# Attention exponentials in triples instead of pairs, with x kept in DRAM meanwhile

## What is computed

```python
q = (x @ Wq.T).reshape(d, n, h)          # d = 128 batches, n = 3327, h = 8
k = (x @ Wk.T).reshape(d, n, h)
v = (x @ Wv.T).reshape(d, n, h)
a = jnp.einsum('dnh,dmh->dnm', q, k) * scale
a = a + adj + adj
a = softmax(a, axis=2)
out = jnp.einsum('dnm,dmh->dnh', a, v).reshape(n, h * d) @ Wo.T
```

## Time and profile before

| | |
|---|---|
| median of three runs | 12,283.2 us |
| the profiled execution, its own time | 12,270.41 us |
| its span, first to last instruction | 12,268.5 us |
| TensorE matmul busy | 11,106.3 us (91%) |
| ScalarE busy | 10,590.3 us (86%) |
| VectorE busy | 10,190.5 us (83%) |
| GpSimd busy | 8,312.7 us (68%) |
| mean granted TensorE clock | 0.959 of 2.4 GHz |
| VectorE's adds (line 1011) | 9,216, 8,980.5 us |
| ScalarE's exponentials of sets (line 966) | 5,120, 7,345.2 us |
| ScalarE's exponentials of GpSimd blocks (line 961) | 4,096, 3,527.3 us |

### The profile page before, as it was taken

How to read it: one execution, slowest core, us unless ns; L and a number is a source line. 1 busy time by engine, 2 the same in 40 slices (tenths; PEclk the granted TensorE clock), 3 DMA queues, 4 the chain that set the end, 5 groups by cost and what they waited for, 6 DMA issues and landing times. The chain is left out here.

```text
span 12268.5 us, 378176 instructions
## 1 busy us (share of the span) xinstructions
PE 11106.3 (91%) x138208; PEld 5172.6 (42%) x138208; DVE 10190.5 (83%) x10283; ACT 10590.3 (86%) x9603; POOL 8312.7 (68%) x4135
## 2 busy tenths in 40 slices
PE   5759999999999999998999999998999999999743
PEld 4524444444444444444343344433343433444721
DVE  6358888888788888887888888888888888888388
ACT  3259999999899999998999999999999999998022
POOL 0017777777677777777777777777777777777023
PEclk7979999999899999999999999999999999999866
DMA  8773333333433333333333333333333333333522
GB/s 315 234 221 58 58 58 58 58 58 58 84 56 58 58 58 58 58 58 66 75 53 54 51 55 52 54 52 66 73 54 52 54 53 53 54 51 58 171 88 75
DMA packets 432583, 943.30 MB, mean 77 GB/s; under 512 B 100728, under 2 KB 349439, under 8 KB 381471
## 3 DMA queue, kind: packets, MB, share of 16 engines
q1 hardware_dynamic: 432508, 942.28, 39.4%
HBM read 799.88 MB, written 142.00 MB: 77 GB/s over the span
## 5 line engine op out<-in xcount | busy, mean ns | idle before, releaser
L1011 DVE SCALAR_TENSOR_TENSOR a_probs<-ps,a_adj 128x768 f32<-128x768 f32 (+1 forms) x9216 | 8980.5, 1020 | 1357.6 <-PE ps L904 1244.9
L986 POOL TENSOR_TENSOR a_pool_probs<-a_pool_probs,a_adj 128x768 f32<-128x768 f32 (+1 forms) x4096 | 8102.3, 1978 | 2382.1 <-ACT a_pool_probs L961 2382.1
L966 ACT ACTIVATE a_probs<-a_probs 128x1536 f32<-128x1536 f32 (+3 forms) x5120 | 7345.2, 1457 | 230.8 <-DVE a_probs L1011 199.8
L904 PE MATMUL ps<-a_q,a_k 34*128 34x512 f32 (+2 forms) x26624 | 4998.3, 413 | 416.0 <-DVE a_probs L1011 258.5
L921 PE MATMUL ps<-a_probs,a_v 128*9 128x192 f32 (+1 forms) x73728 | 4218.9, 341 | 5.3 <-ACT a_probs L966 4.0
L961 ACT ACTIVATE a_pool_probs<-ps 128x768 f32<-128x768 f32 (+1 forms) x4096 | 3527.3, 861 | 58.4 <-PE ps L904 37.4
L904 PEld LDWEIGHTS ps<-a_q,a_k 34*128 34x128 f32 x26624 | 2213.7, 185 | 3139.0 <-DVE a_probs L1011 1183.3
L921 PEld LDWEIGHTS ps<-a_probs,a_v 128*9 128x9 f32 x73728 | 1741.3, 90 | 1747.3 <-ACT a_probs L966 617.0
L921 PE MATMUL ps<-a_pool_probs,a_v 128*9 128x192 f32 (+1 forms) x32768 | 2222.3, 343 | 0.0
L921 PEld LDWEIGHTS ps<-a_pool_probs,a_v 128*9 128x9 f32 x32768 | 488.8, 88 | 1227.1 <-issue 1221.0
L1259 POOL TENSOR_TENSOR e_both<-e_tau,e_nat 128x3328 f32<-128x3328 f32 (+1 forms) x26 | 194.5, 7481 | 701.2 <-DVE e_tau L1297 701.2
(11 more groups left out here) (172 smaller groups left out, 2415.6 us busy)
## 6 DMA issues: line engine op xcount, KB each, us to landing
a_k<-k_parts SPq DMA_DIRECT2D x2048, 208.0 KB
a_v<-v_ext SPq DMA_DIRECT2D x512, 117.0 KB
adj_t<-tr SPq DMA_DIRECT2D x26, 1664.0 KB, 6.4
g0tile<-adj_t SPq DMA_DIRECT2D x26, 1664.0 KB, 6.9
g2tile<-adj_t SPq DMA_DIRECT2D x26, 1664.0 KB, 6.8
nat<-in_adj SPq DMA_DIRECT2D x25, 1663.5 KB, 10.3
e_nat<-in_adj SPq DMA_DIRECT2D x25, 1663.5 KB, 6.9
a_q<-q_parts SPq DMA_DIRECT2D x2048, 16.0 KB
```

The lines of the kernel that those rows point to most:

```text
L904: ins = nc.tensor.matmul(ps[:, slot + begin:slot + end], kt[row:row + SCORE_ROWS, P * j:P * (j + 1)].bitcast(F32R), qt[row:row + SCORE_ROW ...
L966: nc.scalar.activation(both, both, ACT.Exp, scale=2.0).then_inc(sums_exped, 1)
L986: nc.gpsimd.tensor_tensor(probs(k)[:, :, :], probs(k)[:, :, :], adj_c[:, :, j, :], ALU.mult).then_inc(multiplied, 1)
L1011: v.scalar_tensor_tensor(out=probs(k), in0=score(j).rearrange("p (i q) -> p i q", q=P), scalar=SCALE / 2, in1=adj_c[:, :, j, :], op0=ALU.m ...
```

## The change

`sets` is no longer built round the GpSimd blocks: the 18 blocks of VectorE are taken in their order, three at a time. So a batch has six exponentials of three blocks each: (0,2,3), (5,6,8), (9,11,12), (14,15,16), (18,19,21), (22,24,25). The ring still has four slots, now of three blocks (43,008 bytes a partition at 896 columns, 28,672 before). To make room, x is written to DRAM in `projection_phase`, its SBUF tile is freed after that phase, and `output_phase` loads it into a new tile. `weigh_at` follows from `sets`: it becomes {0,2,3} at step 3, {1} at 5, {4,5,6,8} at 8, {7} at 11, {9,11,12} at 12, {10} at 14, {14,15,16} at 16, {13} at 17, {17,18,19,21} at 21, {20} at 24, {22,23,24,25} at 25. The slots of scores, `ahead_by`, the GpSimd blocks and everything else stay.

```diff
+SET = 3
@@ projection_phase
+        x_stored = mem.sem("x_stored")
@@ SyncE of projection_phase
                 sp.dma_start(w[:, n], weight.rearrange("(c h) f -> c h f", h=HEADS)).then_inc(w_loaded, LOAD)
+            sp.dma_start(x_rows, keep.x[:, :, :]).then_inc(x_stored, LOAD)
             for u in range(units):
...
+            sp.wait_ge(x_stored, LOAD)
@@ attention_phase
     if n_pool:
-        alone = [(j,) for j in range(BLOCKS) if not any(abs(j - p) <= 1 for p in pool_blocks)]
-        sets = sorted([(p - 1, p + 1) for p in pool_blocks] + alone)
+        by_dve = [j for j in range(BLOCKS) if not by_pool[j]]
+        sets = [tuple(by_dve[n:n + SET]) for n in range(0, n_dve, SET)]
...
-        dve_ring = mem.sb(name + "probs", [P, ring, 2, nb, P])
+        dve_ring = mem.sb(name + "probs", [P, ring, len(sets[0]), nb, P])
@@ output_phase, SyncE
             sp.dma_start(w[:, :, :].rearrange("p c h -> p (c h)"), wo).then_inc(w_loaded, LOAD)
+            sp.dma_start(x[:, :, :], x_rows).then_inc(x_loaded, LOAD)
@@ output_phase, VectorE
             v.tensor_copy(w_t[:, :, :].rearrange("p h f -> p (h f)"), ps[:, 0:QCOLS]).then_inc(w_copied, 1)
+            dve.wait_ge(x_loaded, LOAD)
             with dve.Fori(0, BLOCKS // 2) as t:
@@ program
+    x_rows = scratch("x_rows", (P, BLOCKS, F))
...
+        with ExitStack() as x_stack:
+            keep.x = Memory(nc, x_stack).sb("x", [P, BLOCKS, F])
+            setup_phase(nc, keep, x, b0, b2, att_src, att_dst, o_rows)
...
+            projection_phase(nc, keep, (wq, wk, wv), (q_parts, k_parts), (q_norms, k_norms), v_ext, x_rows)
...
+        keep.x = Memory(nc, stack).sb("x_again", [P, BLOCKS, F])
+        output_phase(nc, keep, wo, o_rows, x_rows)
```

More of the change, by code:

```diff
@@ L390, in _, with projection_phase @@
             layer_norm_root(nc, act, norm)
-def projection_phase(nc, keep, weights, parts_of, norms_of, v_ext):
+def projection_phase(nc, keep, weights, parts_of, norms_of, v_ext, x_rows):
     with ExitStack() as stack:
@@ L1019, in _, with output_phase @@
                 finish(1, (c + 1) * BATCHES)
-def output_phase(nc, keep, wo, o_rows):
+def output_phase(nc, keep, wo, o_rows, x_rows):
     x = keep.x
@@ L1034, in output_phase @@
         norm = Norm(mem, "wo")
+        x_loaded = mem.sem("x_loaded")
         w_loaded, w_turned, w_copied = mem.sem("wo_loaded"), mem.sem("wo_turned"), mem.sem("wo_copied")
@@ L1333, in __init__ @@
         self.ps = mem.stack.enter_context(mem.nc.psum_tensor("ps", [P, 8 * BANK], F32))
-        self.x = mem.sb("x", [P, BLOCKS, F])
         self.ident = mem.sb("ident", [P, P])
@@ L1353, in program @@
         keep = Kept(Memory(nc, stack))
[L1354 to L1357, removed]
+        with ExitStack() as x_stack:
+            keep.x = Memory(nc, x_stack).sb("x", [P, BLOCKS, F])
+            setup_phase(nc, keep, x, b0, b2, att_src, att_dst, o_rows)
+            adjacency_phase(nc, keep, adj, adj_t)
+            gcn_phase(nc, keep, adj_t, w0, keep.deg0, keep.bias0, True)
+            projection_phase(nc, keep, (wq, wk, wv), (q_parts, k_parts), (q_norms, k_norms), v_ext, x_rows)
         with ExitStack() as bound_stack:
@@ L1374, in program @@
                 attention_phase(nc, keep, group, POOL_BLOCKS, adj_t, k_parts, q_parts, q_shift, v_ext, o_rows)
-        output_phase(nc, keep, wo, o_rows)
+        keep.x = Memory(nc, stack).sb("x_again", [P, BLOCKS, F])
+        output_phase(nc, keep, wo, o_rows, x_rows)
         gcn_phase(nc, keep, adj_t, w2, keep.deg2, keep.bias2, False)
```

## The result

The changed kernel takes 18,218.8 us (median of four runs, 18,190.2 to 18,230.7) against 12,294.0 us of the kernel before: 1.482 times as long, 95% interval 1.478 to 1.486. The forecast was 18,250 us, the range 16,150 to 19,700. The profiled run took 18,230.7 us.

The account below looks back on a forecast made before the run. The prediction took ScalarE, nearly always busy in attention, as the bound. It summed 1,940 + 10 + 256 x (32.6 + 31.1) = 18,257, say 18,250 us, range 16,150 to 19,700.

Parts of the forecast that it names:

- What bounds the kernel: Steady attention before the change: ScalarE busy 2346.51 of 2430 us and 2642.11 of 2680 us, 19.13 and 21.22 us per batch.
- The instructions: ScalarE in attention: six triples replace eight pairs and two singles, saving 195 us over 512 batches if ScalarE never waits.
- The ring: Attention: waits through all engines make batches of 29.64 and 26.20 us, adding 3,965 us at full clock.
- legs: Stretches from one triple's exponential to the next; wide tiles at full clock: 6.82, 3.40, 5.13, 6.82, 7.47 us.
- W's place: TensorE's weighing of a set, claimed to stand in front of the next scores; 1.25 us for three blocks in wide tiles.
- E's place: ScalarE's exponential of a set, claimed to stand ahead of a GpSimd block's exponential; 2.34 us for a wide triple.
- The clock: TensorE in attention: idle gaps bring 1.2 GHz, 42% of wide and 66% of narrow time; 32.6 and 31.1 us per batch.
- S(20): TensorE's scores of block 20; TensorE was forecast idle about 2 us before it in wide tiles.
- x in DRAM: Storing x after the projections and loading it for the output: 10 us taken, bounds 0 to 2 x 7.
- The signs to look for: Profile after: 3,072 set exponentials, ScalarE idle 3,500 us or more before them, TensorE waits, attention clock 0.6 to 0.9.
- Rival A: TensorE keeps full clock throughout attention, so the time is 16,250 us; chance 14%.
- Rival C: ScalarE stays the bound and grouping saves 195 us, giving 12,090 us, if the ring is under 20.9 us; chance 3%.

Follow-up runs that it names:

- kernel of nine pairs: Kernel before (x in SBUF) with nine pairs for eight pairs and two singles, other GpSimd blocks, new steps for exponentials and weighings: 12,160.1 us, ratio 0.9904.
- kernel with fillers: Changed kernel, with TensorE multiplying zeros into the accumulator ahead of the scores of blocks 7, 16 and 20: 16,801.2 us, ratio 1.368.
- the pairs: Changed kernel with VectorE's 18 blocks taken in order two at a time, ring of six slots of two blocks, x in DRAM: 16,850.8 us, ratio 1.372.
- the run with x alone: Changed kernel with the old eight pairs and two singles and a ring of pairs again, x still in DRAM: 12,296.1 us, ratio 1.0016.

## Why the prediction was right

**What bounds the kernel: right.** ScalarE was the bound and its cover was all but complete; the kernel of nine pairs, with ScalarE full, shows how little there was to gain.

**The instructions: right and small.** The triple takes 2,446 ns where 2.45 us was worked out, and no run contradicts 0.1 us for an instruction saved.

**The ring: right.** Forecast legs for wide tiles at full clock were 6.82, 3.40, 5.13, 6.82, 7.47 us. The trace has 6.65, 3.29 and 4.96 for the first three and, in the kernel with fillers, 6.66 and 7.41 for the fourth and the last; so each was put up to 0.2 us too high. A batch at full clock was put at 29.64 and 26.20 us and takes 28.96 and 25.71, the order's loss at 3,965 us and is 3,670. That W's place and E's place make the legs is shown by moving each. Size is not needed for a loss, as the pairs show, but it is a term of the legs: E is in them with 2.34 us for a triple and 1.59 for a pair.

**The clock: the mechanism right, its share too small.** I had put the low clock at 66% of the time in narrow and 42% in wide tiles. The granted clock of 0.64 means (1 - 0.64) / 0.5 = 72% and 0.72 means 56%. This share was chosen from stretches at the chunks' starts and not derived; it was the softest step. Low in both, it met legs that were put too long, and in narrow tiles its price was too high: with the measured shares and legs, the prediction's prices (33.6 and 36.6 us for a batch all low) give 31.4 us for a narrow and 33.2 for a wide batch. Forecast were 31.1 and 32.6, measured 30.3 and 33.3. The sum came within 0.2% because 256 x (-0.8 + 0.7) is close to zero, and not because each term was that good; that was luck. The pairs show how wide the real uncertainty was: there the same reasoning missed by 850 us beyond its upper end. The waits that were to pull the clock down were put somewhat long: 2 us ahead of S(20) and 1.6 ahead of S(16), where the timeline has 1.63 and 1.38. And the prediction took each long gap as the start of a low stretch; the gap of 1.38 us was followed by none, and in the kernel with fillers the clock fell without a gap over 0.5 us in the 8 us before. Fillers in TensorE's waits lower the share of low time; what else sets it stays open.

**x in DRAM: right.** 10 us, 0 to 14 forecast; 20 us, 0 to 39 measured.

**The signs to look for.** 3,072 exponentials of sets, an idle time before them of 5,018 us (3,500 or more forecast), waits of TensorE ahead of S(7) and S(20) for X, and a clock of 0.61 to 0.79 in attention (0.6 to 0.9 forecast) are all there. So is the wait ahead of S(16). Rival A (full clock, 16,250 us) was within 550 us of the kernel with fillers. Rival C (ScalarE stays the bound) is right for nine pairs and wrong for triples: the point from which it decides was put at 20.9 us for the ring.

The Trainium skill ("Perfetto Trace Analysis", Optimizing Scalar/DVE Operations) has beside its rule on grouping a second one: if ScalarE isn't saturated but causes bubbles on other engines, breaking instructions up may let work finish sooner. The triples turned the first case into the second, 99% busy into 64%, and breaking them up again in the run with x alone brought the time back to 12,296 us.

## What to carry to other kernels

Before grouping instructions on a full engine, write down for each engine its program order around the group, and follow from one grouped instruction to the next through every wait: if the round is longer than the engine's own work in it, grouping loses, however much overhead it saves. A small loss by order can bring a larger one when TensorE's clock falls (1.9 us a batch became 12.4 in the narrow tiles of the pairs), so a leg of the ring is to be costed at both clocks, and a kernel to be judged by batches at full clock and by its mean. The nine pairs, with each group behind the instruction that frees the next buffer, gained 1.0%; how much of that grouping gave is not shown.

## What the runs showed of the hardware

- TensorE's clock follows more than its busy time in the profile. In the narrow tiles of the kernel with pairs it was granted 0.53 over a window of 1000 us with TensorE busy 992 us (0.50 through 100 us in which it was busy throughout), and in the kernel of nine pairs 1.00 with 983 us.
- The length of the last gap doesn't tell whether the clock falls. In the changed kernel S(20) at 12034.56 came 1.63 us after TensorE's work before it and found 1.2 GHz, and S(16) at 12029.60 came after 1.38 us and found 2.4 GHz. In the kernel with fillers the clock fell at 12036 with no gap over 0.5 us in the 8 us before. In the wide tiles of the pairs it was 1.00 from 12018 to 12042, with a gap of 1.32 us in it.
- Multiplying by zeros keeps the clock up: with it the clock over the whole span went from 0.694 to 0.892, and the time fell by 1,418 us.
